# Attention and feed-forward in one kernel: K turned and stacked by DMA, the query's norm on VectorE, the last sum split over ScalarE and GpSimd

## What is computed

```python
def xattn(memory, query, b, seq_len):            # 16 heads of 8
    Q  = split_heads(query) * 8 ** -0.5
    logits = einsum('bhqd,bhkd->bhqk', Q, Kh) + b + mask(seq_len)
    return einsum('bhqk,bhkd->bhqd', softmax(logits), Vh)
def ffn(x, w_gate, w_up, w_down):                # 128 -> 512 -> 128
    gate = silu(bitlinear(x, w_gate)); up = bitlinear(x, w_up)
    return bitlinear(gate * up, w_down)          # bitlinear: 8-bit rounding by row, ternary weights
x = x + xattn(ctx, layernorm(x), b, seq_len)
x = x + ffn(layernorm(x), w_gate, w_up, w_down)
```

## Time and profile before

| | |
|---|---|
| median of 3 runs | 181.34 us (181.11 to 182.14) |
| the profiled execution's own time | 181.3 us |
| its span, first to last instruction | 179.2 us |
| busy: TensorE, VectorE, ScalarE, GpSimd | 141.4, 148.7, 130.6, 142.1 us |
| DMA | 9.61 MB, mean 54 GB/s |

### The profile page before, as it was taken

How to read it: one execution, slowest core, us unless ns; L and a number is a source line. 1 busy time by engine, 2 the same in 40 slices (tenths; PEclk the granted TensorE clock), 3 DMA queues, 4 the chain that set the end, 5 groups by cost and what they waited for, 6 DMA issues and landing times. The chain is left out here.

```text
span 179.2 us, 6662 instructions
## 1 busy us (share of the span) xinstructions
PE 141.4 (79%) x2211; PEld 89.2 (50%) x2211; DVE 148.7 (83%) x519; ACT 130.6 (73%) x197; POOL 142.1 (79%) x274
## 2 busy tenths in 40 slices
PE   0015999999998998999999995667777888988562
PEld 0013776666666665666666663112345454555441
DVE  0446767889979898988988888899999999999972
ACT  0005788988978897988888887856785989987541
POOL 7387978889867997888899999998999846774430
PEclk9999999999999999999999999555597999999985
DMA  1999993000000000000000000000001111111222
GB/s 41 308 286 299 287 294 80 4 0 5 5 4 0 5 4 2 4 4 4 0 7 4 4 2 4 2 0 2 0 15 32 46 29 46 49 44 29 60 77 59
DMA packets 16353, 9.61 MB, mean 54 GB/s; under 512 B 1088, under 2 KB 15424, under 8 KB 16320
## 3 DMA queue, kind: packets, MB, share of 16 engines
q1 hardware_dynamic: 15600, 8.39, 17.6%
q10 hardware_dynamic: 720, 0.80, 1.3%
HBM read 7.09 MB, written 2.10 MB: 51 GB/s over the span
## 5 line engine op out<-in xcount | busy, mean ns | idle before, releaser
L517 ACT ACTIVATE probs<-scores,bias_all 128x1024 f32<-128x1024 f32 x64 | 68.5, 1112 | 2.9 <-PE scores L633 2.4
L650 PE MATMUL outs<-probs,v_ones 128*32 128x128 f32 x1024 | 41.9, 283 | 0.1
L618 PE MATMUL turned<-ident_h,k_parts 128*128 128x128 f16 x128 | 19.3, 230 | 15.9 <-DVE q_parts L821 13.6
L650 PEld LDWEIGHTS outs<-probs,v_ones 128*32 128x32 f32 x1024 | 24.7, 111 | 9.0 <-issue 5.8
L633 PE MATMUL scores<-stacks 32*128 32x128 f16 x512 | 26.1, 224 | 1.4 <-DVE stacks L829 1.3
L445 POOL TENSOR_SCALAR hr<-h,h_fac 128x512 f32<-128x512 f32 x32 | 21.9, 692 | 6.5 <-DVE h_fac L910 6.2
L553 ACT ACTIVATE hqT<-turned 128x512 bf16<-128x512 int16 x32 | 19.1, 596 | 8.4 <-PE outs L719 7.7
L829 DVE COPY stacks<-turned 128x512 f32<-128x512 f32 x32 | 21.4, 670 | 4.2 <-PE turned L620 4.1
L546 ACT ACTIVATE silu_g<-scores,gate_s 128x512 f32<-128x512 f32 x32 | 22.0, 688 | 1.6 <-PE scores L691 0.6
L618 PEld LDWEIGHTS turned<-ident_h,k_parts 128*128 128x128 f16 x128 | 12.6, 102 | 19.9 <-issue 16.0
L898 DVE TENSOR_REDUCE h_peak<-h 128x1 f32<-128x512 f32 x32 | 21.5, 672 | 0.0
(11 more groups left out here) (81 smaller groups left out, 293.7 us busy)
## 6 DMA issues: line engine op xcount, KB each, us to landing
result<-x_all SPq DMA_DIRECT2D x32, 64.0 KB, 1.5
k_all<-in_ctx SPq DMA_DIRECT2D x1, 1024.0 KB, 10.8
v_all<-in_ctx SPq DMA_DIRECT2D x1, 1024.0 KB, 10.9
x_all<-in_x SPq DMA_DIRECT2D x1, 512.0 KB, 7.7
k_all<-in_ctx SPq DMA_DIRECT2D x1, 512.0 KB, 7.0
v_all<-in_ctx SPq DMA_DIRECT2D x1, 512.0 KB, 7.1
x_all<-in_x SPq DMA_DIRECT2D x2, 128.0 KB, 5.5
k_all<-in_ctx SPq DMA_DIRECT2D x2, 128.0 KB, 6.6
```

Of the source, the lines that this page charges most:

```text
L517: act.activation(probs[:, p, 8 * a:8 * a + 8, :].rearrange("p h q -> p (h q)"), scores[:, HALF * a:HALF * (a + 1)], ACT.Exp, bias=bias_all ...
L618: pe.transpose(turned_h[:, g * 128:(g + 1) * 128], k_parts[:, p4, heads, :, :].rearrange("p h c d -> p (h c d)"), ident_h[:, :])
L650: last = pe.matmul(sums_ps(p)[32 * g:32 * (g + 1), 128 * r:128 * (r + 1)], pair[:, 32 * i:32 * (i + 1)], probs[:, p, GROUPS * (2 * r + i) ...
```

## The change

K is given to the kernel already turned (features on the partitions, `k_turned` is features x batches x tokens), V as an array of its own. GpSimd splits K's turned tile into high and low for four batches at once. Then SyncE writes both parts to a scratch array in device memory (`k_put`) and reads them back four times, once for each of the four rows per feature, with every fourth partition as destination (`k_get`), so that K's stack stands in SBUF (`k_stacks`) without a transpose. TensorE turns only the query, and `stack_out` copies 256 words instead of 512. `q_norm` goes from GpSimd to VectorE as one scalar_tensor_tensor and `minus1_of` goes. `finish` is split: ScalarE scales `down`'s result into a tile `ffn` (`ffn_out`), GpSimd adds it to x. The order numbers of nearly all stages are new.

```diff
-LAST = 56
-VERDICT = 84
+LAST = 58
+VERDICT = 82
 ...
-        k_parts = sb("k_parts", [128, 4, HEADS, 4, HD], F16)
-        q_parts = sb("q_parts", [128, 4, HEADS, 4, HD], F16)
+        kT_parts = sb("kT_parts", [128, 4, 2, 4, S], F16)
+        k_stacks = sb("k_stacks", [128, 4, GROUPS, 4, S], F16)
+        q_parts = sb("q_parts", [128, 4, D, 4], F16)
+        k_scratch = nc.dram_tensor("k_scratch", [B // 4, D, 2, 4 * S], F16, kind="Internal").ap()
 ...
-                sp.dma_start(k_all[:, a:b, :], ctx[a:b, :, 0:D].rearrange("b s d -> s b d")).then_inc(k_in[i], 16)
-                sp.dma_start(v_all[:, a:b, :], ctx[a:b, :, D:2 * D].rearrange("b s d -> s b d")).then_inc(v_in[i], 16)
+                sp.dma_start(kT_f[:, a:b, :], k_turned[:, a:b, :]).then_inc(k_in[i], 16)
+                sp.dma_start(v_all[:, a:b, :], v[a:b].rearrange("b s d -> s b d")).then_inc(v_in[i], 16)
+
+            def k_put(t, k):
+                quad = t.value(k) // 4
+                sp.wait_ge(k_lo, t.count(k))
+                sp.dma_start(k_scratch[quad].rearrange("r c n -> r (c n)"),
+                             kT_parts[:, quad % 4, :, :, :].rearrange("p c b s -> p (c b s)")).then_inc(k_put_done, 16)
+
+            def k_get(t, k):
+                quad = t.value(k) // 4
+                sp.wait_ge(k_put_done, 16 * (quad + 1))
+                if t.has(k - 16):
+                    sp.wait_ge(scored[1], t.count(k - 16))
+                for part in range(4):
+                    sp.dma_start(k_stacks[part:128:4, quad % 4, :, :, :].rearrange("r g b s -> r g (b s)"),
+                                 k_scratch[quad, :, part % 2, :].rearrange("(g r) n -> r g n", g=GROUPS)).then_inc(k_got, 16)
 ...
+                t.run_quad(k_put, -3)
+                t.run_quad(k_get, -3)
                 t.run(store, -LAST)
 ...
+                pool.tensor_copy(kT_parts[:, slot, 0, :, :], kT_f[:, t.at(k, 4), :]).then_inc(k_hi, 4)
 ...
+                pool.tensor_tensor(kT_parts[:, slot, 1, :, :], kT_f[:, t.at(k, 4), :], kT_parts[:, slot, 0, :, :],
+                                   ALU.subtract).then_inc(k_lo, 4)
 ...
-                qh = q_f[:, p, :].rearrange("p (h o d) -> p h o d", o=1, d=HD)
-                pool.tensor_copy(q_parts[:, p, :, 0:4:3, :], qh.broadcast_to([128, HEADS, 2, HD])).then_inc(q_hi, 1)
+                once = q_f[:, p, :].rearrange("p (d o) -> p d o", o=1)
+                pool.tensor_copy(q_parts[:, p, :, 0:4:3], once.broadcast_to([128, D, 2])).then_inc(q_hi, 1)
 ...
+            def finish(t, k):
+                pool.wait_ge(filled, 4)
+                pool.wait_ge(ffn_done, t.count(k))
+                xb = x_all[:, t.at(k), :].rearrange("p b d -> p (b d)")
+                pool.tensor_tensor(xb, xb, ffn[:, t.side(k), :], ALU.add).then_inc(finished, 1)
 ...
+            def ffn_out(t, k):
+                act.wait_ge(downed, t.count(k))
+                act.wait_ge(out_s_done, t.count(k))
+                if t.has(k - 2):
+                    act.wait_ge(finished, t.count(k - 2))
+                act.activation(ffn[:, t.side(k), :], outs[t.side(k)][:, 256:384], ACT.Copy, scale=out_s[:, t.slot(k)]).then_inc(ffn_done, 1)
 ...
                 for g in range(GROUPS):
-                    heads = slice(PLACES * g, PLACES * (g + 1))
-                    pe.transpose(turned_h[:, g * 128:(g + 1) * 128],
-                                 k_parts[:, p4, heads, :, :].rearrange("p h c d -> p (h c d)"), ident_h[:, :])
-                    last = pe.transpose(turned_h[:, (GROUPS + g) * 128:(GROUPS + g + 1) * 128],
-                                        q_parts[:, p4, heads, :, :].rearrange("p h c d -> p (h c d)"), ident_h[:, :])
+                    last = pe.transpose(turned_h[:, g * 128:(g + 1) * 128],
+                                        q_parts[:, p4, ROWS * g:ROWS * (g + 1), :].rearrange("p d c -> p (d c)"), ident_h[:, :])
 ...
                 pe.wait_ge(stack_done, t.count(k))
+                b = t.value(k)
+                pe.wait_ge(k_got, 16 * GROUPS * (b // 4 + 1))
 ...
+            def q_norm(t, k):
 ...
+                dve.scalar_tensor_tensor(q_f[:, t.side(k, 4), :], x_all[:, t.at(k), :].rearrange("p b d -> p (b d)"),
+                                         mean1[:, t.at(k), 0:1].rearrange("p b o -> p (b o)"),
+                                         rstd1[:, t.at(k)].broadcast_to([128, D]), ALU.subtract, ALU.mult).then_inc(q_done, 1)
 ...
-                dve.tensor_copy(stacks[:, p, :, :, :].rearrange("p a g s -> p (a g s)").bitcast(F32), turned[p][:, :]).then_inc(stack_done, 1)
+                dve.tensor_copy(stacks[:, p, :, :].rearrange("p g s -> p (g s)").bitcast(F32), turned[p][:, 0:256]).then_inc(stack_done, 1)
 ...
-                dve.scalar_tensor_tensor(xb, outs[t.side(k)][:, 256:384], out_s[:, t.slot(k)], xb, ALU.mult, ALU.add).then_inc(finished, 1)
```

More of the change, by code:

```diff
@@ L493, in batch @@
             def batch(t, b):
-                for stage in (vare1_of, rstd1_of, v_beside_ones, vare2_of, rstd2_of, x_round, h_round):
+                for stage in (vare1_of, rstd1_of, v_beside_ones, vare2_of, rstd2_of, x_round, h_round, finish):
                     t.run(stage, 0)
@@ L586, in batch @@
                 heads_of(act, b, head)
-                for stage in (sums_of, xqT_out, silu_of, hqT_out):
+                for stage in (sums_of, xqT_out, silu_of, hqT_out, ffn_out):
                     t.run(stage, 0)
@@ L610, in stack_turn @@
                     pe.wait_ge(idents, 2)
-                pe.wait_ge(k_lo, t.count(k))
                 pe.wait_ge(q_lo, t.count(k))
@@ L632, in score @@
                         col = (GROUPS * place + g) * 128
-                        last = pe.matmul(scores[:, col:col + 128], stacks[rows, p, 0, g, :], stacks[rows, p, 1, g, :],
+                        last = pe.matmul(scores[:, col:col + 128], k_stacks[rows, b // 4 % 4, g, b % 4, :], stacks[rows, p, g, :],
                                          start=True, stop=True)
@@ L659, in sum_a @@
                     pe.wait_ge(attn_done, t.count(k - 2))
+                if t.numbers is None and t.value(k) == W_BATCH:
+                    w_total_of(t, k)
                 sum_half(t, k, 0)
@@ L961, in _ @@
                     verdict_of()
-                t.run(x1_of, -9)
-                t.run(stats1_of, 0)
-                t.run_pair(minus1_of, -1)
-                t.run(stats2_of, -9)
-                t.run(mean2_of, -11)
-                t.run(stack_out, -5)
-                t.run(mean1_of, 0)
-                t.run(denom_of, -8)
-                t.run_quad(minus2_of, -12)
-                t.run(q_low, -4)
-                t.run(attn_of, -8)
-                t.run(h_peak_of, -47)
-                t.run_quad(h_factor, -48)
-                t.run_quad(x_factor, -33)
-                t.run(h_of, -46)
-                t.run_quad(out_scale, -52)
-                t.run(finish, -56)
-                t.run_quad(gate_scale, -34)
+                t.run(x1_of, -12)
+                t.run(q_norm, -6)
+                t.run(stats1_of, -1)
+                t.run(mean1_of, -2)
+                t.run(mean2_of, -13)
+                t.run(stats2_of, -12)
+                t.run(denom_of, -11)
+                t.run(stack_out, -8)
+                t.run_quad(minus2_of, -14)
+                t.run(attn_of, -11)
+                t.run(q_low, -7)
+                t.run_quad(out_scale, -50)
+                t.run(h_peak_of, -49)
+                t.run(y_peak_of, -31)
+                t.run_quad(h_unit_of, -49)
+                t.run_quad(floor_of, -37)
+                t.run_quad(gate_scale, -39)
+                t.run_quad(h_factor, -49)
+                t.run_quad(x_factor, -36)
                 t.run_quad(x_unit_of, -32)
-                t.run_quad(floor_of, -34)
-                t.run_quad(h_unit_of, -47)
-                t.run(y_peak_of, -31)
+                t.run(h_of, -47)
             def prepare():
```

188 lines of the change are left out of this document (82 added, 106 removed).

## The result

| | before | changed |
|---|---|---|
| median, same chip, 4 runs each | 181.23 us | 190.97 us (189.88 to 193.56) |
| the profiled execution's own time | 181.3 us | 190.8 us |
| its span | 179.2 us | 188.8 us |
| busy: TensorE, VectorE, ScalarE, GpSimd | 141.4, 148.7, 130.6, 142.1 | 128.6, 141.2, 133.4, 129.4 us |

The ratio is 1.051 [1.0443, 1.0577] (the brackets are its 95% interval). The two profiled executions differ by 9.5 us (181.3 and 190.8), where 5.6 more than before's median had been forecast. Some executions of every kernel here are disturbed and some per cent longer; the ratios leave them out, the medians don't.

A forecast was written before the change was run, and what follows sets the result against it. TensorE was taken to bound the attention and VectorE the late feed-forward. Start +18.3, attention -8.7 and feed-forward -4.0 us gave 186.9 us against the profiled 181.3; own range 183 to 190, with rivals 179 to 191.

The forecast's parts named there:

- the rivals: Whole kernel: write passes loads, 179.5 us (0.13); both paces at floors, 180.3 (0.10); new attention wait, 193.3 (0.10).
- over to the first `h_of`: Last `weigh` to first `h_of`: last sums, weights' casts and ScalarE's table load stay, 7.0 us.
- tail: Last `h_of` to the span's end: 12.4 us as before, two hops replacing `finish` on VectorE, check of sums moved ahead.
- The start: Before the attention: K's first write waits behind queued loads, first `weigh_a` at 34.9 us, 18.3 later; bounds 27.5 and 37.5.
- the write passes the loads: Start: first `k_put` not held by the queue, first `weigh_a` at 27.5, time 179.5 us; chance 0.13.
- Later rounds are hidden: K's later rounds: SyncE needs 5.6 us a round while TensorE uses up four batches in 10.
- The attention's pace: Attention: 2.55 us a batch, bounds 2.47 and 2.8, down from 2.76; 1.5 more for TensorE's idle start.
- cost at nothing: Attention: VectorE's two-SBUF-operand `q_norm` waiting for long GpSimd instructions, set to nothing; about 5 us if 1 us every fourth batch.
- `q_norm` on VectorE: Attention: VectorE stays even at about 2.45 us of work a batch, GpSimd drops to about 2.2.
- The rival of a slower `q_high`: Attention: single-element writes double `q_high` from 0.448, GpSimd needs 2.65, pace 2.75, time 193.3 us; chance 0.10.
- The feed-forward: First to last `h_of`: 47.4 us, 1.60 a batch for 16 and 1.45 for 15; bounds 43.4 and 51.4 (no gain).
- VectorE no longer full: Sign in the feed-forward's changed profile: VectorE not full, ScalarE near 1.45 us a batch.

The follow-up runs named there:

- e1: Changed kernel with write and reads of K's first four batches ahead of the last 24 batches' loads, the next four's before the last 16's: 182.54 us, 0.9986.
- e2: Changed kernel with the write and four reads of K's first four batches issued from ScalarE's queue, loads as they were: 186.95 us, 1.0142.
- e5: Changed kernel with K's first rounds ahead of the following loads and the check of the sums at step 88, loads not cut further: 180.17 us, 0.9932.
- e6: Changed kernel with K's first four rounds before the next loads, last sixteen batches' loads cut in two, check at step 88: 179.32 us, 0.9691.
- e9: Changed kernel with early K rounds, last sixteen batches' loads cut in two, check at step 88 and `k_low` halved: 174.93 us, 0.9623.
- e10: As e9, with 70 and 45 matmuls of no use added on TensorE while it waits for K: 179.51 us, 0.9717.
- e7: Changed kernel with GpSimd's `k_low` cut into two instructions of 256 elements, a step apart: 188.47 us, 1.0371.
- e3_again: Changed kernel with the check of the sums at step 88 instead of 82, second run, on another chip: 186.25 us, 1.0274.
- e8: Changed kernel with `q_norm` back on GpSimd as a tensor_scalar that subtracts the mean: 202.44 us, 1.1192.
- e4: Changed kernel with `finish` back on VectorE in one instruction, without `ffn_out` and GpSimd's sum: 191.52 us, 1.0478.
- e3: Changed kernel with the check of the sums at step 88 instead of 82, run on two chips: 185.72 us (1.0159) and 186.25 us (1.0274).

## Why the prediction was right

The forecast was a slower kernel by way of a late first `weigh`, and that is what happened. The size is another matter: the time came out 190.97, above the forecast's own 183 to 190 and 0.03 us inside the range of 179 to 191 that allowed for the rivals. That it lies inside is luck: none of the rivals came true, and the slowdown was 9.7 us by the medians where 5.6 were forecast. Term by term, against the profiled 190.8 (3.9 above 186.9):

| step | forecast | measured | difference |
|---|---|---|---|
| first `weigh_a` | 34.9 | 34.3 | -0.6 |
| attention, to the end of the last `weigh` | 83.1 | 84.6 | +1.5 |
| over to the first `h_of` | 7.0 | 5.7 | -1.3 |
| feed-forward | 47.4 | 48.9 | +1.5 |
| tail | 12.4 | 15.3 | +2.9 |
| around the span | 2.1 | 2.0 | -0.1 |

*The start* was right as a mechanism and a number: e1 takes the queue position away and the first `weigh` comes 12.3 us earlier, of 17.7. Two of its parts were off and cancelled: the write had landed by 27.4, not 29.5, and the reads, from 27.4 to the first scores at 32.3, took 4.9 instead of 3.5: an issue takes 0.65 us instead of 0.5 (2.59 for four), and the landing 2.8 (page of the changed kernel) instead of 2.0. The rival "the write passes the loads" fell on SyncE's queue; from another one the write passed a load, and the first `weigh` came only 3.2 us earlier (e2). "Later rounds are hidden" held with all the loads ahead of them; moved between the loads they are not (e1, e5, e6, e9, e10).

*The attention's pace* of 2.55 was right as a mean and wrong inside. The steady period is 2.40, under the floor of 2.47 that had been worked out for ScalarE; its instructions overlap a little more than the earlier trace rows let see. Two losses fill most of the gap. `x1_of` and `q_low` are held by `k_low`, and ScalarE then waits 0.43 to 0.62 us, four times; cost at nothing, this was worth 2.6 us by the ratios where `k_low` was halved (e7), 1.9 by the trace. And the first three batches take 3.5 us each, 3.3 over the steady pace in all, where 1.5 had been allowed. In them TensorE's matmuls take 420 ns instead of 278, until about 44 us; in other executions with the same start this lasts longer, until about 47 in e3_again and about 52 in e7.

*`q_norm` on VectorE* was taken as even there and as relief for GpSimd. e8 shows that GpSimd can't take it back in the form that was tried, at 12 us; what the relief is worth against the kernel before's form isn't shown. The rival of a slower `q_high` (0.476 against 0.448) fell.

*The feed-forward* kept 1.58 a batch instead of 1.53: 1.65 in the first 16 (forecast 1.60) and 1.50 in the last 15 (1.45). The forecast's mechanism held at the end, where ScalarE's packed list goes round in 1.48; its sign "VectorE no longer full" did not (20.8 of the last 21.5 us, as ScalarE). One reading was wrong: the 23.24 us of the earlier trace rows begin at 143.60, between two `h_of` (142.69 and 144.49), and hold 14 intervals and not 15, so that before the last 15 ran at 1.61 and the first 16 at 1.70, not 1.55 and 1.76. The whole of 51.4 stands. Against it the gain is 2.5 where 4.0 was forecast; with `finish` back on VectorE (e4) the stretch takes 52.1.

**The mis-sized term is the tail.** "The check of the sums moves ahead of them and no longer holds the last `finish`. I take 12.4" had the move right and its effect the wrong way round. On an engine that runs its list in order, a check placed further ahead waits where its operand isn't there yet, and what is behind it waits too. The order had to be held against VectorE's list: it was ahead of six `hq_turn`, and its row comes after the last `h_peak`. e3, twice, gives the price: 3.1 to 3.4 us by the traces, and a tail of 12.2 and 11.9, the forecast's 12.4.

Open: what halving `k_low` is worth once the order is mended (e9 against e6), the size of the gain of the cut loads, and the stretch at a granted 0.50 behind the waits for later K rounds. e9's profiled execution took 179.4 us, five of its other seven took 173.2 to 175.2, and how long the clock is low in those no trace shows. A kernel with the first round early and no later wait for K was not run.

## What to carry to other kernels

A round trip through device memory costs 2.0 us for the write and 4.9 for four reads by itself, which only the first batch has to wait for, and much more behind other transfers: put the first round ahead of every load that nobody waits for yet, and look at the next rounds again, which then stand between the loads (7 to 9 us from write to reads in e6, even with the last loads cut). With order, cut loads, late check and halved `k_low` the same edits give 0.962 of the time before instead of 1.051. A side task on an in-order engine belongs behind the work of the main line once its operand comes late; look for it on the engine that waits, not on the one that makes the operand. When busy time falls on three engines and the time rises, read the idle stretches first.

## What the runs showed of the hardware

- An issue to a loaded queue holds the issuing engine: 5.15 us for a write behind the loads (5.68 in e1), 0.33 for the same write on an empty queue. All that follows on SyncE waits with it.
- A transfer on another queue can pass queued ones, but slowly beside them (e2): 256 KB issued a microsecond after a load of 1 MB landed 3.2 us ahead of it, in 6.3 us against 2.0 on an empty queue; four reads of 128 KB took 7.8 each against 2.8.
- VectorE's instructions with two operands in SBUF take up to 1.25 us instead of 0.28 beside a GpSimd `tensor_tensor` of 1.16 us, and up to 0.76 when that one is halved. The Trainium skill (GPSIMD Engine Reference, section Specifications) has the two engines share their SBUF interface; the trace agrees.
- TensorE's first matmuls after an idle start take 420 ns instead of 278 while the record grants 1.00, the same as later ones at a granted 0.50, the lower of its two levels (1.2 GHz). With 115 matmuls of no use ahead, the granted clock read 0.50 from 20 to 28 us and the matmuls were no shorter (e10).
- In the middle of the attention, behind a wait of 2.8 us for a DMA, the granted clock read 0.50 for 13 us with TensorE busy for 12.2 of them, and a batch took 4.1 us instead of 2.40 (e6). In the 10 us before, TensorE had been busy for 7.8.
